# Last two tiles' residual copied into their banks, and the second norm's roots made for several tiles at once

## What is computed

```python
x = hidden_states                                       # 1024 tokens x 512
x = layernorm(x + attention(x, qkv_w, out_w, gate_w, norm_w))
x = layernorm(x + ffn(x, ...))

def ffn(x):                                             # 8 LoRA experts of rank 16
    base_out = x @ base_W.T + base_b
    probs = softmax(x @ router_W.T + router_b)          # 15 entries
    topk_p, topk_i = top_k(probs, 8)
    w = sum over k of topk_p[k] * onehot(expert_map[topk_i[k]])
    h = x @ A[e].T                                      # for each expert e
    lora = sum over e of (h * w[e]) @ B[e].T * 2.0
    return base_out + lora
```

## Time and profile before

| | us |
|---|---|
| median of three runs | 993.08 (992.87 to 993.71) |
| the profiled execution | 994.48 |
| its span | 992.7 |
| TensorE busy in the span | 982.8 |
| last product on TensorE ends (in the span) | 986.59 |
| last output issued, landed | 990.17, 992.27 |

### The profile page before, as it was taken

The page is one execution under the profiler, slowest core; times in us unless marked ns, Lnnn a source line. Parts: engine busy times, 40 slices in busy tenths (PEclk is TensorE's granted clock), DMA queues, the critical chain, the costliest instruction groups (busy, mean ns, idle before and its releaser), DMA issues.

```text
span 992.7 us, 15943 instructions
## 1 busy us (share of the span) xinstructions
PE 982.8 (99%) x5569; PEld 862.8 (87%) x5569; DVE 799.5 (81%) x1058; ACT 727.6 (73%) x1261; POOL 458.3 (46%) x426
## 2 busy tenths in 40 slices
PE   9999999999999999999999999999999999999997
PEld 7888998889888898889988898888988899888896
DVE  6667887878867889679877788778886788889877
ACT  6678885788767885788857887577867888587653
POOL 1353464346544463434653465444635345531423
PEclk9999999999999999999999999999999999999999
DMA  6021211211121012212111111210122121110402
GB/s 212 29 64 36 75 37 57 58 44 52 51 65 51 30 52 72 65 35 75 35 58 58 44 52 51 65 51 30 52 71 64 33 78 35 59 52 22 160 12 86
DMA packets 52800, 57.79 MB, mean 58 GB/s; under 512 B 4336, under 2 KB 47728, under 8 KB 52720
## 3 DMA queue, kind: packets, MB, share of 16 engines
q1 hardware_dynamic: 52720, 56.77, 18.3%
HBM read 54.65 MB, written 2.10 MB: 57 GB/s over the span
## 4 chain that ended last, share of the span: by engine, by line
PE 92%; DVE 2%; ACT 2%; issue 1%; DMA 1%; POOL 1%; SPq 0%; POOLq 0%; ACTq 0%; DVEq 0%
PE ps L2032 24%; PE ps L2033 24%; PE ps L2034 23%; PE ps L2026 3%; PE ps L2028 3%; PE ps L2027 3%; PE ps L2129 2%; PE ps L2123 2%; PE ps L2125 2%; PE ps L2124 2%; PE ps L2143 1%; DMA stage<-stream 1%; DVE wl L1201 1%; PE ps L2127 1%; PE ps L2145 1%
## 5 line engine op out<-in xcount | busy, mean ns | idle before, releaser
L1903 POOL TENSOR_TENSOR stage<-stage 128x512 f32<-128x512 f32 x75 | 106.2, 1416 | 352.6 <-DMA stage<-stream 289.7
L2032 PE MATMUL ps<-xh,wh 128*128 128x512 f32 x658 | 260.4, 396 | 1.4 <-ACT stg L517 1.0
L2033 PE MATMUL ps<-xl,wh 128*128 128x512 f32 x658 | 257.1, 391 | 0.0
L2034 PE MATMUL ps<-xh,wl 128*128 128x512 f32 x658 | 256.2, 389 | 0.0
L1201 DVE TENSOR_TENSOR wl<-stage,wh 128x768 fp32r<-128x768 f32 (+3 forms) x183 | 202.6, 1123 | 23.2 <-ACT wh L471 22.1
L471 ACT ACTIVATE wh<-stage 128x768 fp32r<-128x768 f32 (+3 forms) x183 | 147.6, 834 | 12.8 <-POOL stage L1910 6.9
L2032 PEld LDWEIGHTS ps<-xh,wh 128*128 128x128 f32 x658 | 123.7, 188 | 26.7 <-ACT ps L471 2.1
L2034 PEld LDWEIGHTS ps<-xh,wl 128*128 128x128 f32 x658 | 123.6, 188 | 26.7
L2033 PEld LDWEIGHTS ps<-xl,wh 128*128 128x128 f32 x658 | 123.7, 188 | 21.8
L1946 POOL TENSOR_TENSOR sqacc<-sqacc,sq 128x512 f32<-128x512 f32 x64 | 90.6, 1416 | 108.8 <-ACT sq L635 108.8
L471 ACT ACTIVATE ps<-ps 128x512 f32<-128x512 f32 x150 | 87.4, 586 | 52.5 <-PE ps L2034 43.2
(11 more groups left out here) (224 smaller groups left out, 2322.2 us busy)
## 6 DMA issues: line engine op xcount, KB each, us to landing
stage<-stream SPq DMA_DIRECT2D x75, 384.0 KB, 3.4
stage<-stream SPq DMA_DIRECT2D x79, 128.0 KB, 2.1
dec<-decay SPq DMA_DIRECT2D x32, 192.0 KB, 2.5
stage<-stream SPq DMA_DIRECT2D x13, 256.0 KB, 3.2
acc<-xt SPq DMA_DIRECT2D x8, 256.0 KB, 5.9
v<-x SPq DMA_DIRECT2D x8, 256.0 KB, 6.1
out<-v SPq DMA_DIRECT2D x8, 256.0 KB, 2.1
y_home<-lora_router SPq DMA_DIRECT2D x1, 512.0 KB, 5.0
```

The lines of the kernel that those rows point to most:

```text
L1903: nc.gpsimd.tensor_tensor(stage[:, s, 1:5:3, :], stage[:, s, 0:6:5, :], stage[:, s, 7:8, :].broadcast_to([P, 2, U]), ALU.add).then_inc(t_p ...
L2032: nc.tensor.matmul(dst, wt[0], mv_[0], start=start, stop=False, skip_group_check=True)
L2033: nc.tensor.matmul(dst, wt[0], mv_[1], start=False, stop=False, skip_group_check=True)
L2034: return nc.tensor.matmul(dst, wt[1], mv_[0], start=False, stop=stop, skip_group_check=True)
```

## The change

Three things are changed.

- **Banks of tiles 6 and 7** (`IN_BANK` = 6). ScalarE opens them with the tile of `res` instead of the bias, after all column adds (`columns_added` at 4). GpSimd adds the bias to `res` for tiles 5, 6 and 7, not for 5 alone, and waits for all eight turns first. With that the bank holds the whole residual after `lora(t)`. VectorE's two adds for these tiles go; its statistics and its normalize read the bank, and the statistics wait for `ffn_done`.
- **The columns of tiles 4 to 7** are added after `router_top(1)`, not before; the second add (tiles 6 and 7) waits for three bias adds.
- **The roots of tiles 0 to 4** are made for two tiles and then for three, not one by one; `variance` of tile 4 moves ahead of `normalize` of tile 2 on ScalarE.

```diff
+IN_BANK = 6
...
+                if t >= IN_BANK:
+                    act.wait_ge(columns_added, 4)
+                    nc.scalar.activation(ps[:, FFN_BANK[t], :], res[:, t, :], ACT.Copy).then_inc(bias_set, 1)
+                    return
                 act.wait_ge(bias_in, 16)
                 nc.scalar.activation(ps[:, FFN_BANK[t], :], bb, ACT.Copy).then_inc(bias_set, 1)
...
             variance(TT + 3)
+            variance(TT + 4)
             normalize(TT + 2, out_ready)
-            variance(TT + 4)
...
-                if f == OPENED // HG:
-                    dve.wait_ge(bias_added, 1)
                 for b in range(2):
                     t = HG * f + 2 * b
+                    if t + 1 >= OPENED:
+                        dve.wait_ge(bias_added, t + 2 - OPENED)
...
             def statistics(t):
-                dve.wait_ge(ffn_read, t + 1)
-                link(nc.vector.bn_stats(stat[:, t - STATS, :], res[:, t, :]))
+                if t < IN_BANK:
+                    dve.wait_ge(ffn_read, t + 1)
+                    link(nc.vector.bn_stats(stat[:, t - STATS, :], res[:, t, :]))
+                else:
+                    dve.wait_ge(ffn_done, t + 1)
+                    link(nc.vector.bn_stats(stat[:, t - STATS, :], ps[:, FFN_BANK[t], :]))
...
-                nc.vector.tensor_scalar(res[:, t, :], res[:, t, :], mv[:, t - STATS, 0:1], rstd[:, TT + t:TT + t + 1],
+                full = res[:, t, :] if t < IN_BANK else ps[:, FFN_BANK[t], :]
+                nc.vector.tensor_scalar(res[:, t, :], full, mv[:, t - STATS, 0:1], rstd[:, TT + t:TT + t + 1],
...
-            first_columns(1)
             lora_transposed(0)
             router_top(1)
+            first_columns(1)
...
             statistics(5)
-            second_residual(6)
             statistics(6)
-            second_residual(7)
             statistics(7)
...
-            pool.wait_ge(tr_done, OPENED + 1)
+            pool.wait_ge(tr_done, TT)
             pool.wait_ge(hw_done, 2)
-            nc.gpsimd.tensor_tensor(res[:, OPENED, :], res[:, OPENED, :], bb, ALU.add).then_inc(bias_added, 1)
-            for t in range(4):
-                means(TT + t)
-                affine(TT + t)
-            means(TT + 4)
-            affine(TT + 4)
+            for t in range(OPENED, TT):
+                nc.gpsimd.tensor_tensor(res[:, t, :], res[:, t, :], bb, ALU.add).then_inc(bias_added, 1)
+            for t, m in ((0, 2), (2, 3)):
+                means(TT + t, m)
+                affine(TT + t, m)
             root(5, 2)
             root(7, 1)
```

## The result

| | median us (runs) | against before, 95% interval |
|---|---|---|
| kernel before | 993.67 (9) | |
| changed kernel | 996.87 (9) | 1.0029 (1.0015 to 1.0042) |
| changed kernel, second measurement | 996.82 (12), before 994.29 (35) | 1.0028 (1.0019 to 1.0038) |
| changed kernel, third | 996.91 (11), before 994.39 (35) | 1.0022 (1.0012 to 1.0033) |

What follows compares the result with a forecast made beforehand. TensorE, busy 99%, until 986.59 us and then the last tiles' work and outputs were taken to bound the kernel. Six queued outputs end the span at 994.46, 1.76 more; added to 993.08 that gives 994.8 us, range 993.8 to 995.9.

Steps and rivals of the forecast that it cites:

- VectorE's step after the top-8 search: In the second router pass, moving the column adds behind the search starts the next VectorE step 0.23 us later.
- GpSimd's adds beside VectorE: Around 970 us, three bias adds at 1.58 us each end at 972.0 and hold up nothing on VectorE.
- last product on TensorE: TensorE's end stays at 986.59 us, because the earlier 0.23 us delay is absorbed by idle time: zero change.
- wider calls on GpSimd: Second-norm roots for two or three tiles cost no more than for one; up to 0.2 us in the upper bound.
- six outputs, from first packets to last: At the kernel's end, the DMA engines carry the outputs of tiles 2 to 7 at 0.73 us each, 4.38 us together.
- The mechanism: Late grouped roots idle ScalarE, so six outputs follow one another at the DMA engines' pace; 1.76 us more, chance 0.66.
- Rival (a): At the kernel's end, VectorE's earlier last statistics show fully, 0.59 us less, giving 992.5 us; chance 0.06.
- (b): In the output queue, only SyncE's issue pace of 0.54 us binds, giving 994.3 us, or 993.9 at 0.4; chance 0.11.
- (c): In the output queue, piled-up transfers slow to 0.86 us each, six taking 5.17 us, giving 995.6 us; chance 0.13.
- width costs nothing: A GpSimd root of two columns takes 0.721 us against 0.717 for one, so grouping adds no time per call.
- rival (d): Around the second router pass, GpSimd's adds take 2.33 us each and delay VectorE and TensorE, giving 996.4 us; chance 0.04.
- The opening of banks 6 and 7 with the residual: ScalarE's copies into these banks take 0.60 us as before; a 0.23 us slip is absorbed: zero cost.

Runs made afterwards that it cites:

- e4_one_add: Changed kernel without GpSimd's bias adds of tiles 6 and 7, whose bias is then missing; 996.56 us, 1.0024 against the kernel before.
- e0_after: The changed kernel itself in its second measurement, source of its trace; 996.82 us median, 1.0028 against the kernel before.
- e5_add_held: Changed kernel with roots of tiles 0 to 4 one by one and GpSimd's add of tile 7 held until VectorE's row-maximum subtraction is done; 993.54 us, 0.9995.
- e10_first_pair: Kernel before with only the roots of tiles 0 and 1 made in one call, variances in their old places; 1.0021 against the kernel before.
- e2_roots_single: Changed kernel with the roots of tiles 0 to 4 one by one and the variances in their old places; 1.0002 against the kernel before.
- e3_half_outputs: Changed kernel writing only 256 of 512 columns of the outputs of tiles 2 to 7; 995.93 us, 1.0014 against the kernel before.
- e6_fourth_add: Changed kernel with a fourth, useless add of the same form on GpSimd behind the three; 1.0029 against the kernel before.
- e8_after_again: The changed kernel once more, its third measurement and second trace; 996.91 us, 1.0022 against the kernel before.

## Why the prediction was wrong

By its own steps, all times after T (969.24 in the trace of before):

| step | forecast | measured |
|---|---|---|
| VectorE's step after the top-8 search, without the hold | +0.23 | +0.23 (first residual 7.97 in e4_one_add, 7.74 before) |
| GpSimd's adds beside VectorE | 0 | +0.82 on the first residual (8.79), +0.64 on variance 9 (11.91 against 11.27) |
| last product on TensorE | 0 | +0.28 with the hold, 0.01 without |
| wider calls on GpSimd | 0; in the upper bound up to 0.2, a straggling packet included | +0.24 for two tiles, +0.41 for three |
| third-last normalize of ScalarE starts | 18.23 | 19.51 |
| first of six outputs issued | 19.07 | 20.35 |
| six outputs, from first packets to last | 4.38 | 4.3 (991.55 to 995.85) |
| end of the span | 25.22 | 26.30 |
| median of the kernel before, to which the difference is added | 993.08 | 993.67 to 994.39 |

**The mechanism held.** Roots by groups leave ScalarE idle, outputs 2 to 7 pile up behind the last group, and the DMA engines carry them one behind the other at 0.71 us each. SyncE's pace alone, 0.38 to 0.50, would have ended sooner: the last issue at 993.54, 0.80 to its first packets and 0.71 for them make 995.05, and the last packets came by 995.9. What VectorE wins at the last statistics does go in GpSimd's queue: in e0_after they are out 18.56 after T, before 19.02 (0.73 won, 0.28 lost to TensorE's later end), but tile 7's root starts only at 991.16, behind the calls for the other tiles. TensorE's 0.28 is lost in that wait too. Rival (a), the shortened end, fell; even with single roots and the held add the kernel only comes out even (0.9995).

Rivals (b) and (c) fell too: the DMA engines were at full share from 992 to 995, at 365 to 389 GB/s.

**Two terms of the sum failed**, both about GpSimd: 0.65 and 0.64, together the 1.28 by which the first of the six outputs is late against the forecast. Quicker transfers and a shorter way from the last packet to the end of the span gave 0.2 back, so the end of the span is 1.08 later than forecast. The rest of the median's distance from 994.8, 0.95 us, is no step of this sum: 0.6 is the starting value (993.67 and not 993.08), and the medians of the first measurement lie 3.20 apart where the traces have 2.84.

The first is the sentence "width costs nothing". It rested on one row for the roots of the last tiles, 0.721 us for two columns and 0.717 for one. But those read a column of a two-column statistics tile. In the change's own form one, two and three columns take 0.57, 0.72 and 0.89, so the row for a single column stood 0.15 too high and hid the step from one to two; that the layout makes this 0.15 is likely, and no run here changes the layout alone. The forecast had the own form's single root beside it (0.57, used as 0.65 from start to start) and didn't compare the two. With the steps around it a call takes 1.14, 1.38 and 1.55 us, 0.65 more in all, and all of it is on the path: e4_one_add, which has no hold, starts the third-last normalize 18.86 after T, 0.63 later than forecast.

The second is the argument against rival (d), which was the right place with the wrong sufferer. I priced it as slower adds, at 2.33 us each; they took 1.28. What they do is hold VectorE. The row that I read against it, the subtraction at 966.80 with its usual 0.68, shows the other side of the same thing: it had started before the add at 967.05, and the add was the one to wait, hence 1.58 and not 1.28. The trace of before shows both sides elsewhere too (timeline; first VectorE and GpSimd where GpSimd starts later, then where VectorE does):

```profile
163.13 1.23 DVE L1201 TENSOR_TENSOR wl<-stage,wh 128x1024 fp32r<-128x1024 f32 x1 [0.17 <-ACT wh L471]
```

```profile
163.18 2.33 POOL L1903 TENSOR_TENSOR stage<-stage 128x512 f32<-128x512 f32 x1 [8.34 <-DMA stage<-stream]
```

```profile
20.05 1.14 DVE L1201 TENSOR_TENSOR q<-stg,q 128x512 fp32r<-128x512 f32 x1 [0.74 <-ACT stg L517]
```

```profile
19.35 1.29 POOL L1903 TENSOR_TENSOR stage<-stage 128x512 f32<-128x512 f32 x1 [17.65 <-DMA stage<-stream]
```

The add of 2.33 us, which the forecast took for the price of a slow add, is one of 1.29 that comes 0.05 us into a subtraction of 1.23 us. The subtraction at 20.05 takes 1.14 us where 0.68 is usual, since the add runs to 20.64. So the 0.68 that was read against the hold on VectorE had its counterexample in the same trace. To see who would be held I had to ask which of the two starts first. In the changed kernel the third add starts at about 971.0, VectorE's two-input step at 971.10. I had placed the end of the adds at 972.0, 2.8 us after T, and so had the overlap in the sum, but called VectorE's steps there "short". That a step is short doesn't matter when it is held for the rest of the other's. The Trainium skill ("GPSIMD Engine Reference", Specifications) says that GpSimd shares its SBUF interfaces with VectorE's instructions that have two SBUF inputs; the traces agree, with 1.05 us for one step. The forecast cited it and let one row outweigh it.

The 1.05 us of hold come out as 0.82 at the first residual (8.79 against 7.97 without the adds), since without them VectorE waits 0.23 us for ScalarE's copy there; as 0.64 at variance 9; and as 0.6 at the end (26.30 against 25.71). The first residual is 1.05 later than before in all, and variance 9 only 0.64, so the stage has a slack of 0.41: enough for the 0.23 of the forecast, not for the hold.

**What was right in part.** The opening of banks 6 and 7 with the residual shows no cost of its own: with the adds left out the changed kernel takes 25.71 from T and the roots alone 25.73, and in e5_add_held variance 9 and the end of TensorE stand where they stood before, 11.27 and 17.34 after T. Statistics from a bank take 0.67 to 0.70, as from SBUF. A normalize from a bank takes 0.80, not the 0.69 that I took from the adds, and stands 0.72 behind its neighbour, not 0.46; behind the queue it doesn't show. By the Trainium skill ("VectorE: DVE Perf Modes", Why PSUM operands drop a tier) fp32 loses the double rate there; 0.80 against 0.546 agrees. The longer normalizes are probably why e5_add_held gains 0.03 us and not the 0.3 at the lower end of its expectation: its root for tile 7 is made 0.5 us sooner after T than before, but its last three normalizes follow one another, and the last output is issued 20.86 after T, before 20.93. No run has them from SBUF, so this is read from the rows and not shown.

What stays open is the rest between trace and measurement. The e10_first_pair kernel is 1.33 us slower by its trace and 1.2 to 3.1 by its ratio; single traces can't tell more, with 4 us of spread in T itself, whose cause is open.

## What to carry to other kernels

Where work goes out tile by tile at the end of a kernel, think twice before making a group of a step that feeds the outputs: a call for two or three tiles waits for its last tile, and what it holds back comes out at once and meets a queue. Six outputs of 256 KB at 0.71 us each were 4.3 us here, though the last was ready 3 us before its last packets. When an engine is given more work beside a busy one, look for what both need, and ask at each step which one starts first: in these traces the later one waited for the rest of the other's instruction, so its price goes by the other's length, not its own. A price by width is read from the same form of instruction, with the same layout, or kept open to both sides.

## What the runs showed of the hardware

A VectorE instruction with two inputs in SBUF that comes up while GpSimd runs a 128 x 512 add waits for that add: 1.27 to 1.29 us instead of 0.22 in five traces (e0_after, e2_roots_single, e3_half_outputs, e6_fourth_add, e8_after_again), each ending 0.07 to 0.08 us behind the add. It gets in between two queued adds (e6_fourth_add). Reductions, reciprocals and steps with one input in a bank run beside the add at their usual speed (e5_add_held: 0.20, 0.18 and 0.69 us). The other way round, a GpSimd add that comes up during VectorE's 0.68 us subtraction in SBUF took 1.58 us instead of 1.28 in each of these traces. It isn't the idle time ahead that makes such an add long: in the trace of before one that followed 10.99 us of idle time, with only bank steps of VectorE beside it, took 1.30.

In these rows the record of the later one is longer than usual by what is left of the other's instruction less 0.13 to 0.14 us, in both directions. For VectorE: 1.19 left and 1.05 longer at 971.10, 0.59 and 0.46 at 20.05. For GpSimd: 0.43 left and 0.30 longer at 967.05, 1.18 and 1.04 at 163.18.

A root (power) on GpSimd of 128 x 1, 128 x 2 and 128 x 3 takes 0.57, 0.72 and 0.89 us: 0.15 to 0.17 for each further column.

From an output's issue at 990.75 to its first packets, by 991.6, passed 0.8 us; six in a row took 4.3 us, at 365 to 389 GB/s in the stretches at full share.
